# Attention in blocks of 512: scaling the output behind the low part, and a place of its own for each projected half-quad

## What is computed

```python
h = maximum(layernorm(x), 0);  x = x + L0(h, adj)      # a first graph layer, not touched here
h = maximum(layernorm(x), 0);  x = x + L1(h, adj)
# L1: two layers, each with W of 256 x 512 and x of 4096 x 256
proj = x @ W
Wh, Ws = split(proj, 2)
a = softmax(Wh @ Ws.T) * adj                           # 4096 x 4096, adj of zeros and ones
x = leaky_relu(a @ Wh + x)
```

## Time and profile before

| | |
|---|---|
| median of 3 runs | 2607.56 us (2607.18 to 2609.16) |
| the profiled execution's own time | 2606.61 us |
| its span, first to last instruction | 2604.6 us |
| mean granted TensorE clock | 0.983 of full speed |
| TensorE busy with matmuls | 2450.7 us |
| VectorE busy | 2123.9 us |
| ScalarE busy | 1724.9 us |
| POOL busy | 1491.6 us |
| opening of layer 0 (g0a), attention (g0b) | about 917 to 975 us, 975 to 1764 us |
| opening of layer 1 (g1a), attention (g1b) | about 1764 to 1812 us, 1812 us to the end |

### The profile page before, as it was taken

One profiled execution on the slowest core, in us unless ns is written; L12 is line 12 of the kernel. 1 busy time (PEld: TensorE's weight loads), 2 busy tenths in 40 slices (PEclk: granted clock), 3 DMA queues, 4 the chain that ended last, 5 costly groups with the idle time before them and its releaser, 6 DMA issues. The chain is left out here.

```text
span 2604.6 us, 35453 instructions
## 1 busy us (share of the span) xinstructions
PE 2450.7 (94%) x12284; PEld 2042.1 (78%) x12284; DVE 2123.9 (82%) x2773; ACT 1724.9 (66%) x2348; POOL 1491.6 (57%) x892
## 2 busy tenths in 40 slices
PE   6799999999999969999999999977999999999996
PEld 5688888888888867888888888756788888888874
DVE  5899999999999545888888888884688888888887
ACT  5999999999999654555555555653455555555554
POOL 4899999999999700444444444450144454444456
PEclk9899999999999989999999999998999999999999
DMA  3322222222222151556655655676155665566576
GB/s 117 108 94 91 93 95 91 95 93 92 92 94 82 45 188 49 186 165 207 194 176 196 194 181 192 217 251 242 32 181 183 196 206 188 189 206 199 181 239 201
DMA packets 139457, 398.40 MB, mean 153 GB/s; under 512 B 13072, under 2 KB 54800, under 8 KB 137232
## 3 DMA queue, kind: packets, MB, share of 16 engines
q1 hardware_dynamic: 137952, 395.36, 46.8%
q10 hardware_dynamic: 1328, 0.79, 0.1%
HBM read 366.74 MB, written 29.36 MB: 152 GB/s over the span
## 5 line engine op out<-in xcount | busy, mean ns | idle before, releaser
L91 PE MATMUL l0b_acc<-l_h_parts,l0b_turned_hi 128*128 128x512 f32 x1984 | 727.1, 405 | 19.1 <-POOL l0b_turned_lo L614 19.0
L614 POOL TENSOR_TENSOR l0b_turned_lo<-l0b_turned,l0b_turned_hi 128x1024 fp32r<-128x1024 f32 x256 | 614.5, 2418 | 45.3 <-ACT l0b_turned_hi L651 43.4
L92 PE MATMUL l0b_acc<-l_h_parts,l0b_turned_lo 128*128 128x256 f32 x1984 | 558.4, 281 | 0.0
L91 PEld LDWEIGHTS l0b_acc<-l_h_parts,l0b_turned_hi 128*128 128x128 f32 x1984 | 376.0, 190 | 112.2 <-POOL l0b_turned_lo L614 29.2
L1251 POOL TENSOR_TENSOR g0b_sum_wide<-g0b_sum_wide,g0b_slab 128x512 f32<-128x512 f32 x194 | 251.3, 1295 | 275.3 <-DVE g0b_masked_psum L1366 267.5
L1251 POOL TENSOR_TENSOR g1b_sum_wide<-g1b_sum_wide,g1b_slab 128x512 f32<-128x512 f32 x194 | 253.0, 1304 | 247.4 <-DVE g1b_masked_psum L1366 239.1
L92 PEld LDWEIGHTS l0b_acc<-l_h_parts,l0b_turned_lo 128*128 128x128 f32 x1984 | 374.3, 189 | 0.9
L651 ACT CAST l0b_turned_hi<-l0b_turned 128x1024 fp32r<-128x1024 f32 x256 | 268.0, 1047 | 67.3 <-PE l0b_acc L92 50.1
L1283 ACT CAST g_parts<-g1b_masked_psum 128x1024 fp32r<-128x1024 f32 x128 | 130.2, 1017 | 162.1 <-DVE g1b_masked_psum L1366 132.4
L1283 ACT CAST g_parts<-g0b_masked_psum 128x1024 fp32r<-128x1024 f32 x128 | 130.2, 1017 | 158.8 <-DVE g0b_masked_psum L1366 114.1
L80 PE MATMUL g1b_acc<-g_parts,g1b_wh_ring 128*128 128x512 f32 x512 | 202.4, 395 | 17.0 <-issue 15.7
(11 more groups left out here) (251 smaller groups left out, 6043.2 us busy)
## 6 DMA issues: line engine op xcount, KB each, us to landing
g_adj_ring<-in_adj_blocks_dram SPq DMA_DIRECT2D x256, 512.0 KB, 5.0
l_adj_ring<-in_adj_quads_dram SPq DMA_DIRECT2D x128, 512.0 KB, 3.3
g0b_wh_ring<-wh_rows SPq DMA_DIRECT2D x128, 512.0 KB, 4.1
g1b_wh_ring<-wh_rows SPq DMA_DIRECT2D x128, 512.0 KB, 4.2
wh_rows<-g_parts SPq DMA_DIRECT2D x16, 1024.0 KB, 4.9
l0b_x_in<-in_x_dram SPq DMA_DIRECT2D x32, 128.0 KB, 2.1
x_rows<-l0b_x SPq DMA_DIRECT2D x32, 128.0 KB, 2.1
all_early<-x_rows SPq DMA_DIRECT2D x8, 512.0 KB, 6.0
```

The source lines that it names most:

```text
L91: pe.matmul(out, lhs_hi, rhs, start=first, stop=False)
L92: return pe.matmul(out[:, width:], lhs_lo, rhs[:, :width], start=False, stop=False)
L614: pool.tensor_tensor(turned_lo[:, m % PART_RING, :, :], turned[:, m % TURN_RING, :, :], turned_hi[:, m % PART_RING, :, :].bitcast(F32), AL ...
```

## The change

`wh_stage` becomes a buffer of the opening with 16 places, 64 KB a partition, one for each half-quad of the layer. `out_high` no longer waits for a store, and a store no longer waits for the one before. The buffer lies where the attention's `slab` begins, and reaches past it by one half-quad's 4 KB into the first place of `wh_ring`, which SP fills only when all stores have landed. ScalarE now waits for all eight stores before its first copy into `slab` (chunk 4, first tile), and no longer before the high part of chunk 0. In the attention VectorE's drain stands behind the low part.

```diff
+            wh_stage = mem.sbuf("wh_stage", [P, QUADS * OUTS, CHUNK, 2, D], F32R)
             w_hi = mem.sbuf("w_hi", [P, KT, D], F32R)
...
-            STAGES = 2 * OUTS
-            wh_stage = parts[:].rearrange("p a u t n -> p (a u t n)").rearrange(
-                "p (s t h d) -> p s t h d", t=CHUNK, h=2, d=D)
...
             def wh_to(c, o, high):
-                return wh_stage[:, (OUTS * c + o) % STAGES, :, 0 if high else 1, :]
+                return wh_stage[:, OUTS * c + o, :, 0 if high else 1, :]
...
                     def store_wh(c):
                         sp.wait_ge(out_lo_made, OUTS * (c + 1))
-                        wait(sp, wh_stored, 16 * c)
-                        stage = wh_stage[:, (c % 2) * OUTS:(c % 2 + 1) * OUTS, :, :, :].bitcast(F32)
+                        stage = wh_stage[:, c * OUTS:(c + 1) * OUTS, :, :, :].bitcast(F32)
...
                     def out_high(c):
-                        wait(act, wh_stored, 16 * (c - 1))
                         for o in range(OUTS):
...
                         if e == 0:
                             wait(act, summed, CHUNK * (c - SLOTS + 1))
+                        if c == EARLY and e == 0:
+                            act.wait_ge(wh_stored, 16 * QUADS)
                         act.copy(tile_of(c, e), bank("score", CHUNK * c + e)).then_inc(score_taken, 1)
...
                     def high_part(c):
                         act.wait_ge(weighted, c + 1)
-                        if c == 0:
-                            act.wait_ge(wh_stored, 16 * QUADS)
                         wait(act, products, c - 1)
...
                             shift(n - TO_SHIFT)
-                        for k in range(2):
-                            b = block_at(n, TURN_OUT[k])
-                            if b is not None:
-                                drain(b, k)
                         b = block_at(n, Q_AT)
                         if b is not None and b + 1 < BLOCKS:
                             q_low(b + 1)
                         if 0 <= n - TO_SPLIT < CHUNKS:
                             low_part(n - TO_SPLIT)
+                        for k in range(2):
+                            b = block_at(n, TURN_OUT[k])
+                            if b is not None:
+                                drain(b, k)
                         b = block_at(n, TURN_MAX)
```

## The result

The changed kernel takes **2566.54 us** (median of 4 runs, 2564.45 to 2568.77), the kernel before on the same chip 2608.22 us: a ratio of 0.984 (95% interval 0.9823 to 0.9857). The forecast was 2566.3. The profiled execution took 2564.45 us with a span of 2562.7; the span before was 2604.6, so 41.9 us are to be found.

What follows compares the result with a forecast made beforehand. TensorE, busy 94% of the span, was taken as the bound, so gains are its idle or low-clock stretches. 8.5 + 10.5 + 1.3 + 21.0 = 41.3 us off 2607.6 gave 2566.3 us, range 2561 to 2577.

Steps and rivals of the forecast that it cites:

- The openings, 8.5 and 10.5 us: g0a and g1a: with a place per half-quad, copies and stores stop waiting for landings; gains 8.5 and 10.5 us.
- The scaling, 21.0 us: Attention steps with output back: low part fills VectorE's wait for transposes, 24 TensorE idles go; gain 21.0 us.
- the layers' ends: Two drains after the last score: VectorE's same work in another order gains 0, within 1 us either way.
- The clock, 1.3 us: g1b's first two queries: no lower clock once TensorE's idle for the store goes; gain 1.3 us.
- the layers' rest: g0b and g1b after their first two queries: forecast gains of 10.3 and 10.7 us.
- The wait at chunk 4, nothing: ScalarE's added wait for all stores at chunk 4 costs nothing, with 10 and 8 us of cover at 322 GB/s.
- openings give nothing: Rival: stores land some 10 us later than counted, ScalarE stands at chunk 4; 2586.6 us, chance 0.05.
- slower: Rival: queue at 153 GB/s makes ScalarE's wait at chunk 4 cost 60.0 us; 2626.3 us, chance 0.02.
- rows late: Rival: in the openings' last quads, row loads behind stores set the pace, losing 6.0 us; 2572.3 us, chance 0.13.
- SP's queue: SP at the openings' ends: stores go out earlier, and the block's end waits for nothing new.
- The drain halved: Rival: in attention, VectorE's earlier weighting waits for value rows, losing half the scaling's gain; 2576.8 us, chance 0.11.

Runs made afterwards that it cites:

- experiment 6: Changed kernel plus 12 unread matmuls at each opening's end: 2564.1 us; repeated, 2565.4 us beside the unaltered changed kernel's 2566.6 us.
- experiment 5: Changed kernel with ScalarE's wait for all eight stores moved from chunk 4 to its first operation of attention: 2571.9 us, ratio 0.9864.
- drain-only run of experiment 1: Kernel before with only the output's scaling moved behind the low part, ring of four places kept: 2586.8 us, ratio 0.9915.
- first run of experiment 2: Kernel before with TensorE's transposes of the output moved ahead of its weighting, VectorE's order untouched: 2586.5 us, ratio 0.9913.

## Why the prediction was right

**The openings, 8.5 and 10.5 us.** Right: 8.2 and 10.7. g0a's last low part ends at 966.50 (predicted 966.2); g1a, from the end of its weights' preparation to its last low part, takes 36.49 us and took 47.23. Taking the pace from quads that were not yet bound, 4.18 and 3.75 us, was sound, and so was counting the last two quads half by half.

**The scaling, 21.0 us.** Right in mechanism, a little small. The half alone gave 22.0 by medians. In the trace the blocks with the idles gained 11.1 and 11.0 us where 10.3 and 10.7 were predicted, 1.84 us a block with the two scalings and not 1.75. Another 0.5 is an idle of g0b at 1447.8 that went too, and 0.3 and 1.9 us came at the layers' ends, put at 0 within 1. By experiment 6 a layer's end varies about as much between executions of one kernel, so I don't ascribe that part to the change. The run with the transposes moved shows that the loss was the wait in VectorE's queue, as argued.

**The clock, 1.3 us: the term that failed.** The prediction took the clock behind g1a to be low "after TensorE had idled over 5 us for the store", let it recover wholly, and had g0b's queries unchanged. The kernel before's own rows speak against the first part:

```profile
975.48 0.47 PE L80 MATMUL g0b_side_psum<-g_vt_hi,g_mix_hi 128*128 128x512 f32 x1 [2.14 <-PEq L937]
...
1812.21 0.47 PE L80 MATMUL g1b_side_psum<-g_vt_hi,g_mix_hi 128*128 128x512 f32 x1 [2.14 <-PEq L937]
...
1813.78 0.63 PE L80 MATMUL g1b_side_psum<-g_vt_hi,g_mix_hi 128*128 128x512 f32 x1
```

TensorE had idled 4.56 us for the store, and behind that the last quad ran at the low clock. But g1b's queries began at the full clock (0.47 us) and dropped to half of it 1.6 us later, behind a second idle of 2.14 us at the barrier. The change removes the first idle and leaves the second. So nothing was to be gained in g1b (-0.25 us), and g0b's queries, which this execution of the kernel before had run at the full clock, lost 1.58 us. The term is -1.8.

The filler run shows that the short idle is needed for the drop: without it the queries take 5.10 to 5.14 us in both layers of both executions. It is not enough for it. Of all the traces here, 16 openings end with an idle of 2.14 us. Behind 14 of them the clock dropped; behind two it did not, g0b of the kernel before and g0b of experiment 5, whose TensorE does up to there just what it does in the changed kernel:

```profile
965.42 0.47 PE L80 MATMUL g0b_side_psum<-g_vt_hi,g_mix_hi 128*128 128x512 f32 x1 [2.14 <-PEq L935]
...
968.00 0.39 PE L82 MATMUL g0b_side_psum<-g_vt_hi,g_mix_lo 128*128 128x512 f32 x1
```

A last quad at the low clock does not protect the queries either: g1a of the kernel before ended with one (0.50 from 1808 to 1810), as g0a did (0.52 from 970 to 974), and only g0b's queries stayed fast. With openings as in the kernel before, g0b's queries took 6.89 and 6.91 us in the drain-only run of experiment 1 and in the first run of experiment 2. So the 1.58 us may be the luck of one execution and not an effect of the change; against 6.9 us the whole term would be about 0 (an estimate from these two runs). Why two openings were spared stays open.

The Trainium skill (TensorE: Matmul & The Clock Gate, The HAM clock gate) says that idleness closes the gate, and the prediction's sentence on it had named this gap, but only as a reason to leave the 1.3 us out. The trace agrees with the rule in 14 of those 16 openings. The forecast came out within 0.3 us by luck: this error of 3.1 us and that of the layers' rest, 3.8 us too little, cancel.

**The wait at chunk 4, nothing.** Right, with more cover than given: 15 and 13 us, not 10 and 8. The rate was underestimated. 322 GB/s was read in a stretch in which SP still held stores back; with them free the queue moved 375 GB/s over 954 to 966 and 420 to 426 in its fullest parts. That settles the rivals "openings give nothing" and "slower" (which needed some 175 GB/s by the prediction's own sum, where it says 172) and also "rows late": no matmul of the openings waits for rows.

**SP's queue.** The prediction said that the block's end waits for nothing new. That is true, but it did not see that the old wait in SP's queue was a cause by itself: with it alone put back, all 20 us of the openings go. The sum was right because the change removes both waits.

**The drain halved.** It did not happen. VectorE's weighting waits for value rows at the step shown, but by 0.20 us only; over the layers these waits are as before (57.8 and 57.0 us in all, and were 58.5 and 57.6). The idle before the scores' loads is gone in all 24 places.

## What to carry to other kernels

When a ring is replaced by places of their own, look at every queue that waited for it: here the issuing engine's wait for the store before, put back alone, lost all 20 us of the gain, and the short ring alone 15.5 of them. An operation that waits at the head of an in-order queue costs the wait and not its own time; move it behind work that is ready, or make what it waits for earlier, and either gives the same. When a lower clock is put down to an idle, look in TensorE's own rows for where it dropped: here it was behind a second, shorter idle, which the change left. And one trace is not enough to call such an idle harmless.

## What was not expected of the hardware

After an idle of 2.14 us TensorE ran seven matmuls in g0b and eight in g1b at half speed, from about 1 us after its restart on (0.63 and not 0.39 us each). The same idle did so in 14 of 16 openings; 12 matmuls, 1.60 us of work that nobody reads, prevented it in both layers and both executions.

Stores of 1.05 MB that need not wait for each other, with loads between them, moved 375 to 426 GB/s; issued one after the other's landing they went out every 5.0 to 5.5 us, some 200 GB/s for the stores themselves. With three adjacency loads of 0.52 MB ahead of the last four, a store took up to 9.1 and 9.0 us to land (g0a and g1a, two quads' places); with these loads behind all stores it took at most 6.3 and 6.0, and the kernel 5 to 6 us less.
